# One-head graph attentions in groups of two tiles, with the node mask as bits among the scores

## The reference

```python
def _gat_conv(h, W_l, al, ar, b, src, dst, n):
    hp = h @ W_l
    el = hp @ al
    er = hp @ ar
    e = jax.nn.leaky_relu(el[src] + er[dst], NEG_SLOPE)
    emax = jax.ops.segment_max(e, dst, num_segments=n)
    ex = jnp.exp(e - emax[dst])
    denom = jax.ops.segment_sum(ex, dst, num_segments=n)
    alpha = ex / denom[dst]
    out = jax.ops.segment_sum(hp[src] * alpha[:, None], dst, num_segments=n)
    return out + b
```

## Time and profile before

| | |
|---|---|
| median of three runs | 9230.18 us (9221.27 to 9230.35) |
| profiled execution | 9205.22 us |
| its span, first to last instruction | 9203.4 us |
| busy: PE / DVE / ACT / POOL | 5304.3 / 5497.2 / 2663.2 / 5989.4 us |
| mean granted PE clock | 0.801 of full |
| layer 1, first gather to last accumulation | 3454.4 to 4815.7 us |
| layer 2, the same | 4991.5 to 6355.4 us |
| router's attention, first to last gather | 6722.0 to 8420.5 us |

### The profile page before, as it was taken

How to read it: one execution, slowest core, us unless ns; L and a number is a source line. 1 busy time by engine, 2 the same in 40 slices (tenths; PEclk the granted TensorE clock), 3 DMA queues, 4 the chain that set the end, 5 groups by cost and what they waited for, 6 DMA issues and landing times. The chain is left out here.

```text
span 9203.4 us, 106904 instructions
## 1 busy us (share of the span) xinstructions
PE 5304.3 (58%) x25002; PEld 3341.1 (36%) x25002; DVE 5497.2 (60%) x17675; ACT 2663.2 (29%) x6716; POOL 5989.4 (65%) x5966
## 2 busy tenths in 40 slices
PE   0000009732699736777774777774236666544998
PEld 0000008611355424555553555553112222211666
DVE  8889009722122246777765777775279999876222
ACT  0000004311122213333331333331036666543121
POOL 2888777777777767777766777776657777653000
PEclk9999999865899868888887888897655555555999
DMA  5111112100100024444453444444021111686000
GB/s 131 21 22 21 26 20 46 33 2 1 25 1 1 1 36 101 103 103 105 104 83 65 104 102 104 102 104 49 4 13 13 13 13 13 11 10 27 0 0 28
DMA packets 478988, 406.20 MB, mean 44 GB/s; under 512 B 295745, under 2 KB 411192, under 8 KB 478520
## 3 DMA queue, kind: packets, MB, share of 16 engines
q0 software_dynamic: 223232, 306.44, 21.4%
q1 hardware_dynamic: 217656, 77.17, 4.4%
q10 hardware_dynamic: 37632, 17.48, 0.8%
HBM read 345.14 MB, written 55.70 MB: 44 GB/s over the span
## 5 line engine op out<-in xcount | busy, mean ns | idle before, releaser
L715 POOL DMA_INDIRECT G<-tab_gat,pay x2048 | 2024.8, 989 | 711.9 <-issue 602.8
L424 POOL DMA_INDIRECT pay_sorted<-pay,pos x1856 | 1860.1, 1002 | 726.9 <-issue 571.5
L715 POOL DMA_INDIRECT G<-tab_rt,pay x1216 | 1154.3, 949 | 578.8 <-issue 280.5
L793 PE MATMUL pU<-G,PM 128*128 128x257 f32 x4096 | 1268.8, 463 | 3.9 <-DVE acc L1074 3.9
L260 POOL DMA_INDIRECT attr_sorted<-rows,pos x832 | 948.4, 1140 | 412.0 <-issue 253.4
L793 PEld LDWEIGHTS pU<-G,PM 128*128 128x128 f32 x4096 | 882.0, 226 | 209.6 <-issue 17.7
L737 PE MATMUL pA<-identb,G 128*3 128x128 bf16 (+1 forms) x3264 | 394.4, 258 | 913.6 <-DMA G<-tab_gat,pay 605.7
L1578 DVE TENSOR_TENSOR t<-pO,BL 128x1024 f32<-128x1024 f32 (+1 forms) x130 | 151.2, 1163 | 1119.2 <-PE pO L1525 1119.1
L856 ACT ACTIVATE y<-pW,bias 128x512 f32<-128x512 f32 x512 | 352.1, 688 | 1384.4 <-DVE dm L955 1268.8
L818 ACT ACTIVATE aT<-pA 3x512 bf16<-3x512 bf16 (+1 forms) x816 | 471.6, 578 | 863.5 <-PE pA L737 862.7
L760 PE MATMUL pW<-aT,sel 28*128 28x512 bf16 x1216 | 574.3, 624 | 247.7 <-DVE mt L970 247.7
(11 more groups left out here) (292 smaller groups left out, 9959.3 us busy)
## 6 DMA issues: line engine op xcount, KB each, us to landing
G<-tab_gat,pay POOLq DMA_INDIRECT x2048, 2.8
pay_sorted<-pay,pos POOLq DMA_INDIRECT x1856, 2.1
G<-tab_rt,pay POOLq DMA_INDIRECT x1216, 2.5
attr_sorted<-zattr SPq DMA_DIRECT2D x1, 16896.0 KB, 53.5
rows<-attr_sorted ACTq DMA_DIRECT2D x256, 66.0 KB
attr_sorted<-rows,pos POOLq DMA_INDIRECT x832, 2.2
rows<-in_edge_attr_dram SPq DMA_DIRECT2D x51, 256.0 KB, 3.6
tab_gat<-rows SPq DMA_DIRECT2D x24, 518.0 KB, 3.6
```

The source lines that it names most:

```text
L424: pool.indirect_dma_start(out=out, out_offset=bass.IndirectOffsetOnAxis(ap=self.pos[g][:, lo + n:lo + n + 1], axis=0), in_=self.pay[g][:, ...
L715: pool.indirect_dma_start(out=G[:, j, k, 0:R], out_offset=None, in_=table, in_offset=bass.IndirectOffsetOnAxis(ap=pay[:, g, k, 0:1], axis=0))\
L793: ins = nc.tensor.matmul(u[:, 0:F], PM[:, j % 2, k * P:(k + 1) * P], G[:, j, k, 0:F], start=(k == 0), stop=(k == K - 1))
```

## The change

1. **Groups of two tiles.** `KS` gives the groups of each sort: 4 tiles for the adapter and the router, 2 for the one-head layers. Their groups are then 464 (464*2 = 928 tiles) instead of 256 (1024 tiles). `RING` becomes 32 // K: 16 groups of two with one head, 8 of four with four. `pay` is loaded in pieces of K entries, so with one head in 464*128 pieces of 16 bytes where there were 256*128 of 32.
2. **The mask as bits** for one head too: `Nm`, `masks` and the L750 matmuls go, `turn_scores` transposes 20 rows instead of 3, and one matmul of 256 columns makes `pW`. ACT gets `node_bits` (two copies a group).
3. **Bits within the pipeline**, for one head and four: `node_parts` makes one eighth of the bits when a group with `g % PART == 0` comes three steps ahead, where before all were made first.
4. **Negated running maximum.** `m` holds the negated maximum, so that it is ACT's bias without another operation; `maxima` is five small operations behind the reduction where it was seven (and the reduction has 256 columns instead of 512).
5. **Score on ACT.** ACT adds adst and copies to SBUF (`score`, with a register load for the block's number, behind its wait on `s_max`), and DVE's `leaky` works in SBUF, in place: e = max(0.2*e, e). PM is copied by ACT instead of DVE. The lists of parts change accordingly.

```diff
+KS = (K, 2, K)
+NGS = tuple(-(-((e + NB * (k * P - 1)) // (k * P)) // (16 // k)) * (16 // k) for e, k in zip((E0, E0, E1), KS))
+GC = -(-max(NGS) // P)
...
-    NG = NG0 if gi == 1 else NG1
+    NG, K = NGS[gi], KS[gi]
+    RING = 32 // K
...
-                    pe.wait_ge(s_N, g + 1)
                     if g_ge(g, 2):
                         pe.wait_ge(s_e, g - 1)
-                    w = pW[j % 2]
-                    nc.tensor.matmul(w[:, :], sel[:, 0, :], aT[:, j % 2, :], start=True, stop=False)
-                    for k in range(K):
-                        ins = nc.tensor.matmul(w[:, k * P:(k + 1) * P], Nm[:, j, k, :], low[:, :],
-                                               start=False, stop=(k == K - 1))
-                    ins.then_inc(s_W, 1)
+                        pe.wait_ge(s_max, g - 1)
+                    nc.tensor.matmul(pW[j % 2][:, 0:K * P], sel[:, 0, :], aT[:, j % 2, :], start=True, stop=True).then_inc(s_W, 1)
...
-            def sloped(g, j, turn):
-                act.wait_ge(s_W, g + 1)
-                act.wait_ge(s_tab, g + 1)
+            def score(g, j, turn):
+
+                act.wait_ge(s_max, g + 1)
                 if g_ge(g, 2):
-                    act.wait_ge(s_e, g - 1)
-                a.activation(y[:, j % 2, :], pW[j % 2][:, :], ACT.Identity, bias=bias[:, j % 2, 0:1], scale=SLOPE)\
-                    .then_inc(s_y, 1)
+                    act.wait_ge(s_PT, g - 1)
+                act.reg_load(group_node[j % 4], grp[0:1, g:g + 1])
+                ad = adst[:, bass.ds(act.snap(group_node[j % 4], min_val=0, max_val=NB - 1), 1), 0]
+                a.activation(e[:, j % 2, :], pW[j % 2][:, 0:K * P], ACT.Identity, bias=ad).then_inc(s_y, 1)
+
+            def copy_weights(g, j, turn):
+                act.wait_ge(s_turned, g + 1)
+                if g_ge(g, 2):
+                    act.wait_ge(s_U, g - 1)
+                a.activation(PM[:, j % 2, :], pP[:, 0:K * P], ACT.Copy).then_inc(s_PM, 1)
...
-                pipeline(act, NG, [(0, sloped), (0, rescale), (2, copies), (0, weights)])
+                pipeline(act, NG, [(0, score), (0, rescale), (2, copies), (3, node_bits), (-2, copy_weights), (0, weights)], RING)
...
+            def node_parts(g, j, turn):
+
+                if g % PART == 0:
+                    nodes(v.tensor_copy(nodei[:, :, :], pay[:, g:g + PART, :, 1].bitcast(F32)))
+                    for n in range(8):
+                        nodes(v.tensor_scalar(bit[:, :, :], nodei[:, :, :], n, 1, ALU.logical_shift_right, ALU.bitwise_and))
+                        nodes(v.tensor_copy(bits[:, g:g + PART, :, n], bit[:, :, :]))
...
-                v.scalar_tensor_tensor(e[:, s, :], pW[s][:, :], adst[:, bass.ds(blk, 1), 0], y[:, s, :],
-                                       ALU.add, ALU.max).then_inc(s_e, 1)
...
+                v.scalar_tensor_tensor(e[:, j % 2, :], e[:, j % 2, :], SLOPE, e[:, j % 2, :], ALU.mult, ALU.max).then_inc(s_e, 1)
...
-                pipeline(dve, NG, [(-2, copy_weights), (0, maxima), (3, masks), (-4, accumulate), (0, leaky)])
+                pipeline(dve, NG, [(3, node_parts), (0, maxima), (0, leaky), (-4, accumulate)], RING)
             else:
-                pipeline(dve, NG, [], several_heads)
+                pipeline(dve, NG, [(3, node_parts)], RING, several_heads)
```

More of the change, by code:

```diff
@@ L612, in g_ge, with pipeline @@
     return not isinstance(g, int) or g >= n
-def pipeline(eng, n, parts, whole=None):
+def pipeline(eng, n, parts, RING, whole=None):
     least, most = min((a for a, _ in parts), default=0), max((a for a, _ in parts), default=0)
     if whole:
-        least = -4
+        least, most = min(least, -4), max(most, 0)
     for it in range(-most, n - least):
@@ L651, in attention @@
         pay = sb("pay", [P, NG, K, 2], I32)
-        node = sb("node", [P, NG, K], BF16)
         G = sb("G", [P, RING, K, RW])
-        Nm = sb("Nm", [P, RING, K, P], BF16)
+        SPREADS, PART = H if one else H + 1, NG // 8
+        sel, selT = sb("sel", [ROWS, SPREADS, P], BF16), sb("selT", [P, SPREADS, ROWS], BF16)
+        bits, nodei, bit = sb("bits", [P, NG, K, 8], BF16), sb("nodei", [P, PART, K], I32), sb("bit", [P, PART, K], I32)
+        rowf, rowb = sb("rowf", [P, 1]), sb("rowb", [P, BITS])
         rown = sb("rown", [P, 1], I32)
@@ L692, in attention @@
                              "s_tab", "s_alpha", "s_U", "s_acc"))
+        s_low = sem("s_lowest") if one else None
+        s_bits, s_sel, s_node = sem("s_bits"), sem("s_sel"), sem("s_node")
         if one:
@@ L720, in _ @@
         def _(pe):
[L721 to L726, removed]
+            pe.wait_ge(s_sel, 1)
+            for h in range(SPREADS):
+                ins = nc.tensor.transpose(pA[:, h * P:(h + 1) * P], selT[:, h, :], self.identb[:, :])
+            ins.then_inc(s_sel, 1)
+            pe.wait_ge(s_sel, 3)
             pe.wait_ge(s_set, NSET)
@@ L732, in turn_scores @@
                     pe.wait_ge(s_aT, g)
-                if not one:
-                    pe.wait_ge(s_bits, g + 1)
+                pe.wait_ge(s_bits, g + 1)
                 parts = G[:, j, :, SP0:RW].bitcast(BF16)
@@ L808, in _ @@
             act.wait_ge(s_ld, 16)
-            if not one:
-                act.wait_ge(s_sel, 2)
-                a.activation(sel[:, :, :].rearrange("r h p -> r (h p)"), pA[:, :], ACT.Copy).then_inc(s_sel, 1)
-                act.wait_ge(s_set, NSET)
+            act.wait_ge(s_sel, 2)
+            a.activation(sel[:, :, :].rearrange("r h p -> r (h p)"), pA[:, 0:SPREADS * P], ACT.Copy).then_inc(s_sel, 1)
+            act.wait_ge(s_set, NSET)
             def copies(g, j, turn):
@@ new lines, in _ @@
+            c(v.memset(selT[:, :, :], 0.0))
+            c(v.memset(rowb[:, :], 0.0))
+            for n in range(7):
+                c(v.tensor_scalar(bit[:, 0, 0:1], rown[:, :], n, 1, ALU.logical_shift_right, ALU.bitwise_and))
+                c(v.tensor_copy(rowf[:, :], bit[:, 0, 0:1]))
+                c(v.tensor_copy(rowb[:, 8 + n:9 + n], rowf[:, :]))
+                c(v.tensor_scalar(rowb[:, n:n + 1], rowf[:, :], -1.0, 1.0, ALU.mult, ALU.add))
+            c(v.memset(rowb[:, 7:8], 1.0))
@@ L912, in _ @@
+            for h in range(SPREADS):
+                if h < H:
+                    for q in range(3):
+                        v.memset(selT[:, h, q * H + h:q * H + h + 1], 1.0)
+                v.tensor_scalar(selT[:, h, BIT0:], rowb[:, :], -BIG if h < H else -1.0, None, ALU.mult)
+            c(v.tensor_scalar(rowf[:, :], self.rowid[:, :], 0.0, None, ALU.add))
+            dve.sem_inc(s_sel, 1)
+            if not one:
                 c(v.tensor_copy(ad3[:, :, 0, :], adst[:, :, :]))
```

133 lines of the change are left out of this document (44 added, 89 removed).

## The result

| | before | after |
|---|---|---|
| median | 9225.73 us (9217.99 to 9230.35, 4 runs) | 8930.74 us (8928.80 to 8932.95, 4 runs) |
| ratio, 95% interval | | 0.9681 (0.9664 to 0.9698) |
| span of the profiled execution | 9203.4 us | 8927.0 us |
| mean granted PE clock | 0.801 | 0.808 |

The kernel is 3.2% faster; 8952 was predicted, 21 us too much. The rows of the changed kernel that answer those of before come first.

What follows compares the result with a forecast made beforehand. POOL's gather pitch was taken to bound the one-head stage. Twice (-140+16.5-8) = -263, four heads -16, sorts +1: -278 us, from 9205.22 to 8927, plus 25 to the median: 8952 us, range 8880 to 9130.

Steps and rivals of the forecast that it cites:

- The anchor: Whole program: 278 us saved from the profiled 9205.22 gives 8927; the median lies 25 above, so 8952 us.
- Real tiles: One-head layers: 880 tiles at 1.25 us, 1100, plus 22 for stretched gathers: 1122 against 1262, -140 a layer.
- rival (b): One-head layers: e falls on a gather's start in each group, 0.3 us instead of 0.05: 9172 us; chance 0.10.
- DVE 2.28: One-head layers: DVE's operations for a group of two sum to 2.28 us, 2.4 with node bits, under 2.50.
- rival (a): One-head layers: a second engine sets the rhythm, 2.75 us a group, 88 more a layer: 9128 us; chance 0.12.
- The register load: ACT's queue, behind the wait for the maximum: costs 0 to 0.8 us, taken as hidden up to some 0.5.
- rival (c): One-head layers: PE's clock sinks to its low level, 2.95 us a group, 176 more a layer: 9304; chance 0.05.
- Rival (d): One-head layers: pay loads no slower and e never meets a gather, 37+44 us less: 8871 us; chance 0.05.
- Loading pay: Before a one-head layer's first gather: cost goes by pieces, 59392 take 38.0 us, +16.5 a layer.
- Padding and drain: End of each one-head layer: 48 padding tiles keep their time, the 16 us drain halves, -8 a layer.
- Four heads: Four-head stage: bits made in the pipeline start it 49 us earlier, five parts cost 33: -16, ends -3 and -46.
- Start of the program: The sorts before the layers get a fourth column of group counts: +1 us.

Runs made afterwards that it cites:

- the second trace: The kernel before, unchanged, run again with a profile of its own: 9228.00 us, ratio 0.9999.
- pm_on_dve: The changed kernel with the copy of PM given back from ACT to DVE: 9236.04 us, ratio 1.0008 to the kernel before.
- pay_kept: The changed kernel with one-head pay loaded once and kept in SBUF for the second layer: 11276.21 us on a slower chip, where the kernel before took 11373.6.
- best: The changed kernel with padding entries naming distinct table rows and one-head pay kept in SBUF for the second layer: 8738.33 us, ratio 0.9469 to the kernel before.
- bits_first: The changed kernel with the router's bits all made before its pipeline: 11335.21 us on a slower chip, where the kernel before took 11373.6.
- two_alone: The kernel before with groups of two tiles in the one-head layers and nothing else changed: 9403.63 us, ratio 1.0192.

## Why the prediction was right

**The anchor.** The sum was made against the first trace of before, and 25 us were added for the distance to the median. Against that trace the change saves 276.4 us (278 predicted). Against the second trace, which is at the median, it saves 299.4, 21 more than the sum, and that is the 21 us by which the prediction was high. The 276.4 lies so near 278 by luck: the real tiles gave 20 us more than was summed, and the padding stretches took 21 us longer than in that one execution (16 in the router, 5 in the two layers), where the sum had them unchanged. The 25 us that were added for its distance to the median were mostly the same padding. Against the second trace, which the points below use, the sum's terms missed by: real tiles 21 us too little gained, the start of the program and the stages between 7, four heads 6 too much, pay and drain 0.4 together.

**Real tiles: right in kind, the stretching sized too dear.** 1262.9 and 1265.1 became 1114.9 and 1112.2, -148 and -153 (-140 predicted). 880 tiles at 1.25 us are 1100; what gathers stretched by e add was sized at 22 and is 13.0 and 10.9. The stretched gathers are few (71 and 62 of 880) and lose at most 0.25 us: their starts have to fall into some 0.12 us of DVE's 2.32. Lockstep, rival (b), did not come: DVE's 2.32 us and POOL's 2.50 drift against each other.

**DVE 2.28: right** (2.32), with the bits' 0.11 still under 2.50. Two experiments show how thin the margin was: 0.33 us more is the whole gain (rival (a), 9128 predicted; 9236 in fact, with the clock lower too), and 0.18 more is 51 us.

**The register load: hidden, as taken, but not whole.** In the group above the reduction ends at 4151.36 and ACT starts the score at 4151.93; by the median over all groups of the layer the distance is 0.44 us, and DVE's e waits 0.1 a group for it. DVE's slack carries that.

**The clock, rival (c): did not come.** 0.94 in the stage, not 0.50. Its price for a low group, worked out as 3.08 less some 0.13 for the masks, was a little low: in pm_on_dve such a group takes 3.08. Rival (d) did not come either: pay is slower, and e meets gathers.

**Loading pay: right.** 37.1 and 36.9 us against 38.0 predicted; pieces count, not bytes. pay_kept and best show it from the other side: without the load 36.2 us go.

**Padding and drain: right.** 85.3 and 85.2 us against 84.9 and 85.6; the drain 8.5 and 9.7 against 15.9 (-8 predicted). That padding is slow by its own row was not asked.

**Four heads: the failed term.** -16 was predicted, from the pay issue to the end of the program it is -10.0 (+3.8 against the first trace). The first reduction comes 52 us earlier, as the sum had it (49; its own price of 6.6 us for each of the seven parts that moved gives 46, and its end for all of them hidden, -46, does not fit its 49 either). But by the 889th gather only 10 us are left, since a part made in the running pipeline costs 7.8 us, not 6.6 (38.9 us more from the 5th to the 223rd reduction, for five parts), and the first four groups take 3.4 us longer. The two parts in the padding are nearly free, as predicted: 544.8 and 545.5 us against 543.2. bits_first, which puts them back, loses 14 us, on the slower chip.

**Start of the program.** pay of layer 1 is issued 4.9 us earlier, where the sorts were to cost 1; nothing was run on this.

## What to carry to other kernels

Halving the granule of a padded, gather-bound loop pays by the padding it removes only if each other engine's sum per new, smaller group is under the gathers' time for it; add the fixed costs up per group first, since here the same edit alone lost 1.9%. An engine that is just at the pitch (2.50 of 2.50) is already too slow, as it can't catch up after a periodic extra, and a gain that rests on so thin a margin can be gone on a slower chip. Give padding entries distinct rows: what they fetch doesn't matter when it is weighted with zero, but that they all fetch the same does. And before a sum is anchored to one trace, see where that execution lies among the runs.

## What the runs showed of the hardware

- Gathers that all read one and the same row of DRAM with all their 128 entries keep the DMA engines busy 0.88 of the time at 10 GB/s and land after 13.6 us; with distinct rows it is 0.13 at 13 GB/s and 2.4 us.
- An in-place VectorE operation with both inputs from one SBUF tile stretches an indirect DMA that POOL starts 0.05 to 0.17 us after it (0.95 to 1.18 us); with one of the inputs in PSUM it doesn't (0.95).
- A direct load in pieces of 16 bytes costs by the piece, as one of 32 bytes does: 59392 pieces in 37.1 us, 32768 in 21.5.
- In front of a VectorE operation whose scalar operand is addressed by a register stood 0.13 us of idle time that no wait explains (71.8 us less 9.3 of waits, 464 times); before its counterpart with fixed addresses, which reads SBUF alone, it was 0.03 (60.4 less 45.8). Both stand behind short operations. Behind the accumulation of 0.48 us, in two_alone, the same kind of operation (L1062) had under 0.01 (2.5 us in all, 464 times), so that time can be hidden.
- One and the same program differed by 13.7 us in one stretch of padding between two executions (529.5 and 543.2), perhaps on different chips.
